# The output projection of a scan as f16 halves with a factor per chunk, one step later

## What is computed

```
x = x + 0.5 * _L0_ffn_ref(_layernorm(x, axis=-1), ...)
x = x + _L0_attn_ref(_layernorm(x, axis=-1), ...)
x = x + 0.5 * _L0_ffn_ref(_layernorm(x, axis=-1), ...)

def _L0_attn_ref(hidden_states, ...):
    h = rmsnorm(hidden_states, ln1_w)
    h = res + mamba2(h, w_in, conv_w, conv_b, A_log, D, dt_bias, w_out)
    h2 = rmsnorm(h, ln2_w)
    return h + silu(h2 @ gate_w.T) * (h2 @ up_w.T) @ down_w.T

def mamba2(...):
    ...
    y = Y.reshape(B, L, D_INNER) * silu(z)
    return y @ w_out.T
```

## Time and profile before

| | before |
|---|---|
| three runs, us | 766.61, 768.95, 770.06 |
| median, us | 768.95 |
| profiled execution, us | 768.65 |
| its span, us | 766.9 |
| PE busy in the span, us | 755.4 |
| DVE, ACT, POOL busy, us | 626.5, 446.4, 337.2 |
| the scan's sixteen steps, us from the span's start | 87.38 to 333.00 |

### The profile page before, as it was taken

One profiled execution on the slowest core, in us unless ns is written; L12 is line 12 of the kernel. 1 busy time (PEld: TensorE's weight loads), 2 busy tenths in 40 slices (PEclk: granted clock), 3 DMA queues, 4 the chain that ended last, 5 costly groups with the idle time before them and its releaser, 6 DMA issues.

```text
span 766.9 us, 10654 instructions
## 1 busy us (share of the span) xinstructions
PE 755.4 (98%) x3469; PEld 353.2 (46%) x3470; DVE 626.5 (82%) x1230; ACT 446.4 (58%) x881; POOL 337.2 (44%) x392
## 2 busy tenths in 40 slices
PE   8999999999999999999999999999999999999998
PEld 3444554454555444444443444444444444444443
DVE  6888878878878979878799978878878878767994
ACT  3877767766686766643545556456456456444441
POOL 5631534663442379775413333233233233224574
PEclk9999999999999999999999999999999999999999
DMA  8843543552321211420521743743743743443565
GB/s 311 171 75 71 139 94 83 110 111 60 78 56 28 42 38 42 114 55 1 124 47 23 172 77 64 163 77 62 164 77 65 162 77 66 79 77 69 119 169 138
DMA packets 95414, 71.86 MB, mean 94 GB/s; under 512 B 65232, under 2 KB 72400, under 8 KB 95360
## 3 DMA queue, kind: packets, MB, share of 16 engines
q0 software_dynamic: 17280, 31.46, 23.0%
q1 hardware_dynamic: 77600, 39.66, 19.5%
q10 hardware_dynamic: 480, 0.07, 0.1%
HBM read 20.32 MB, written 4.19 MB: 32 GB/s over the span
## 4 chain that ended last, share of the span: by engine, by line
PE 77%; DVE 13%; ACT 4%; issue 3%; POOL 2%; DMA 1%; ACTq 0%; POOLq 0%; DVEq 0%
PE PS L1960 64%; PE PS L2083 4%; PE PS L2183 3%; DVE raw L1450 2%; PE PS L2091 1%; DVE stage L1450 1%; PE PS L2056 1%; DVE state L1432 1%; PE PS L2065 1%; DVE st L1289 1%; PE PS L2073 1%; PE PS L2048 1%; DVE xs L1382 1%; DVE S L1415 1%; DMA h<-lora_b_t 1%
## 5 line engine op out<-in xcount | busy, mean ns | idle before, releaser
L712 POOL DMA_DIRECT2D xs<-x x59 | 50.9, 864 | 151.2 <-ACT x L1159 137.1
L1960 PE MATMUL PS<-h,w_in 128*128 128x512 f16 x480 | 108.7, 379 | 0.2 <-issue 0.2
L1960 PE MATMUL PS<-h,x_t 128*128 128x512 f16 x408 | 94.0, 379 | 0.0
L1960 PEld LDWEIGHTS PS<-h,w_in 128*128 128x128 f16 x480 | 46.9, 98 | 65.3 <-issue 15.5
L1960 PE MATMUL PS<-n_T,stage 128*128 128x512 f16 x288 | 71.5, 379 | 0.0
L1159 ACT ACTIVATE x<-PS,d_d 128x512 f32<-128x512 f32 x59 | 40.2, 682 | 39.1 <-PE PS L1960 39.1
L1960 PEld LDWEIGHTS PS<-h,x_t 128*128 128x128 f16 x408 | 39.5, 98 | 48.5 <-issue 2.3
L521 POOL TENSOR_TENSOR r<-mv,mhalf 128x1 f32<-128x1 f32 (+1 forms) x32 | 29.4, 917 | 72.2 <-DVE mv L1293 55.0
L712 POOL DMA_DIRECT2D xs<-n x29 | 25.2, 868 | 71.1 <-ACT n L1159 60.8
L1960 PE MATMUL PS<-pre,stage 128*128 128x512 f16 x192 | 49.3, 379 | 0.0
L1129 ACT ACTIVATE xds<-tm,dgh 128x512 f32<-128x512 f32 x24 | 17.3, 722 | 53.0 <-DVE tm L1889 53.0
(11 more groups left out here) (314 smaller groups left out, 1819.3 us busy)
## 6 DMA issues: line engine op xcount, KB each, us to landing
xs<-x POOLq DMA_DIRECT2D x75, 256.0 KB, 3.3
xs<-n POOLq DMA_DIRECT2D x29, 256.0 KB, 3.3
x_t<-x_in SPq DMA_DIRECT2D x16, 256.0 KB, 3.0
x_t<-hb POOLq DMA_DIRECT2D x16, 256.0 KB, 3.8
out<-x_t SPq DMA_DIRECT2D x16, 256.0 KB, 2.3
raw_gu<-gate_t SPq DMA_DIRECT2D x7, 512.0 KB, 4.4
raw_gu<-up_t SPq DMA_DIRECT2D x7, 512.0 KB, 6.6
raw_d<-down_t SPq DMA_DIRECT2D x7, 512.0 KB, 7.3
```

Source lines behind the costliest of these rows:

```text
L712: po.dma_start(chunk_of(xs, c), d_tmps[d % 3], accum_op=ALU.add).then_inc(s_acc[d % 3], 16)
L1960: ins = pe.matmul(out_, lhs(a, b, k), rhs(a, b, k), start=first and n == 0, stop=last and n == len(todo) - 1)
```

## The change

`w_out` is held as two f16 halves, scaled by a power of two, and so is y, for which each chunk and row finds a factor of its own. ACT squares y and sums over its columns (`y_sum`), PE sums over the partitions and spreads the sum (`y_over`, a matmul 128x1), DVE reads it (`y_max`), POOL takes powers (`y_scale`: the factor and its inverse), ACT makes the high half (`y_hi`) and DVE the low one (`y_lo`). The projection `w(c)` becomes one `product` of twelve f16 matmuls, and `residual2` multiplies by the inverse factor.

This chain takes longer than the step has room for, so w(c-1) is done in step c, and `residual2`, `square`, `renorm`, `rms2`, `hi2`, `lo2` and `t2` of a chunk each move one step later. `s2_inner(c)` now waits for `y_max(c-1)`, which reads the bank that it writes. In the steps 12 to 15, `y_max`, `y_hi` and `y_lo` of a chunk stand in its own step, w still in the next, and w(15) behind the first gate/up product after the scan. In the prologue the raw `w_out` is loaded later and to another place, and ACT and DVE make its scale and halves (`wo_sum`, `wo_scale`, `wo_hi`, `wo_lo`). Some links between instructions of one engine take another form.

```diff
-        w_out = sb("w_out", [P, H, DM])
+        w_out = sb("w_out", [P, 2, H, DM], F16)
 ...
+            if c > 0:
+                put(("w", c - 1), (e_x2, c), None if i + 1 < NS else B_P[2])
             if i + 1 < NS:
-                put_proj(i + 1, SLOTS[j][0])
+                for q in SLOTS[j]:
+                    put_proj(i + 1, q)
 ...
+            def y_scale(c):
+                po.wait_ge(e_ym, c + 2)
+                po.tensor_tensor(y_s[:, c, :], y_m[:, c, :], halves[:, :], ALU.pow).then_inc(e_yscale, 1)
 ...
+            def y_sum(c):
+                ac.wait_ge(e_y, c + 1)
+                if c > 1:
+                    ac.wait_ge(e_ssq, c - 1)
+                ac.activation(junk[:, :].rearrange("p (h t) -> p h t", h=H), y_of(c), ACT.Square, accum_out=ssy[:, c:c + 1]).then_inc(e_ysum, 1)
+
+            def y_hi(c):
+                ac.wait_ge(e_yscale, c + 1)
+                if c > 0:
+                    ac.wait_ge(e_wo, c)
+                ac.activation(y_hl[:, 0, :, :], y_of(c), ACT.Copy, scale=y_s[:, c, 0:1]).then_inc(e_yhi, 1)
 ...
+            def y_max(c):
+                ve.wait_ge(e_yall, c + 1)
+                ve.tensor_scalar(y_m[:, c, :], PS[:, B_SS, 0:1].broadcast_to([P, 2]), Y_TINY, None, ALU.max).then_inc(e_ym, 1)
+
+            def y_lo(c):
+                cols = slice((c % CH) * P, (c % CH + 1) * P)
+                ve.wait_ge(e_yhi, c + 2)
+                ve.scalar_tensor_tensor(y_hl[:, 1, :, :], szs[(c // CH) % 2][:, :, cols], y_s[:, c, 0:1], y_hl[:, 0, :, :],
+                                        ALU.mult, ALU.subtract).then_inc(e_ylo, 1)
 ...
-                ve.tensor_tensor(x2[:, j % 2, :], n1[:, :], bank(PLAN["w", c][0]), ALU.add).then_inc(e_x2, 1)
+                ve.scalar_tensor_tensor(x2[:, j % 2, :], bank(PLAN["w", c][0]), y_s[:, c, 1:2], n1[:, :], ALU.mult, ALU.add).then_inc(e_x2, 1)
 ...
+                if 0 < c <= 3 * CH:
+                    y_max(c - 1)
                 if c == 2 * CH + 2:
                     bound_row(0)
 ...
+                    y_lo(c - 1)
                     slot_b(i_late, late[0])
 ...
             def w(c):
                 b, freed = PLAN["w", c]
-                y = szs[(c // CH) % 2]
-                if c == 0:
-                    pe.wait_ge(s_wout, 16)
-                pe.wait_ge(e_y, c + 1)
+                pe.wait_ge(e_ylo, H + c + 1)
                 pe.wait_ge(*freed)
-                for h in range(H):
-                    last = pe.matmul(bank(b), y[:, h, (c % CH) * P:(c % CH + 1) * P], w_out[:, h, :], start=h == 0, stop=h == H - 1)
-                last.then_inc(e_wo, 1)
+                product(bank(b), lambda a, b, h: y_hl[:, a, h, :], lambda a, b, h: w_out[:, b, h, :], H).then_inc(e_wo, 1)
+
+            def y_over(c):
+                pe.wait_ge(e_ysum, c + 2)
+                pe.wait_ge(e_state, c + 1)
+                pe.matmul(PS[:, B_SS, 0:1], ssy[:, c:c + 1].broadcast_to([P, P]), over[:, :], start=True, stop=True).then_inc(e_yall, 1)
 ...
                     s1_bc(c + 1)
+                if c > 0:
+                    w(c - 1)
                 if i + 1 < NS:
                     proj(i + 1, SLOTS[j][0])
 ...
-                w(c)
                 if c == 2 * CH + 2:
                     csm(i + 1)
 ...
-                    for q in SLOTS[j][1:]:
+                    for n, q in enumerate(SLOTS[j][1:]):
                         proj(i + 1, q)
+                        if n == 0:
+                            y_over(c)
```

More of the change, by code:

```diff
@@ L209, in build @@
         wv = sb("wv", [P, 2, H])
+        y_hl = sb("y_hl", [P, 2, H, P], F16)
+        over = sb("over", [P, 1])
+        halves = sb("halves", [P, 2])
+        ssy = sb("ssy", [P, NCH])
+        y_m = sb("y_m", [P, NCH, 2])
+        y_s = sb("y_s", [P, NCH, 2])
+        wo_s = sb("wo_s", [P, 4])
         PS = ctx.enter_context(nc.psum_tensor("PS", [P, 8, 512], F32))
@@ L574, in _ @@
             chain(po.memset(ones3[:, :], 1.0))
+            chain(po.memset(over[:, :], 2.0 ** (-2 * Y_TOP)))
+            chain(po.memset(halves[:, 0:1], -0.5))
+            chain(po.memset(halves[:, 1:2], 0.5))
             chain(po.memset(ident[:, :], 0.0))
@@ L715, in _ @@
                 step(c)
-            for n in range(4, N_TOP):
+            rms2(NCH - 2, CH - 2)
+            for n in range(2):
+                t_op(2, n)
+            rms2(NCH - 1, CH - 1)
+            for n in range(2, N_TOP):
                 t_op(2, n)
@@ L939, in step @@
                     slot_b(i_late, late[0])
+                if 0 < c <= 3 * CH:
+                    y_hi(c - 1)
                 if a + 1 < NCH:
@@ L954, in step @@
                     hi1(a, a % CH)
+                y_sum(c)
                 if c + 1 < NCH:
@@ L969, in step @@
                     gate_a(0, j)
+                    y_hi(c)
                     gate_b(0, j)
-                square(c, j)
+                if c > 0:
+                    square(c - 1, (c - 1) % CH)
                 if i + 1 < NS:
@@ L1417, in scan1, with wo_scale, wo_lo @@
                 last.then_inc(e_S, 1)
+            def y_max(c):
[6 more added lines that the diff above has]
+                                        ALU.mult, ALU.subtract).then_inc(e_ylo, 1)
+            def wo_scale():
+                top, pw_, sw_, back = (wo_s[:, n:n + 1] for n in range(4))
+                ve.wait_ge(e_ysum, 1)
+                power_of_two(pw_, sw_, top, chain)
+                chain(ve.tensor_scalar(back, pw_, d_ih[:, :], 2.0 ** -W_TOP, ALU.mult, ALU.mult))
+                ve.sem_inc(e_ym, 1)
+            def wo_lo(h):
+                ve.wait_ge(e_yhi, 1)
+                ve.scalar_tensor_tensor(w_out[:, 1, h, :], wo_raw[:, h, :], wo_s[:, 2:3], w_out[:, 0, h, :],
+                                        ALU.mult, ALU.subtract).then_inc(e_ylo, 1)
             def gate_y(c, j):
@@ L1731, in step @@
                 else:
+                    y_max(c)
                     gate_up(0, j)
-                if j != 2 or i + 1 == NS:
-                    residual2(c, j)
+                    y_lo(c)
                 if c == 3 * CH:
@@ L1806, in _ @@
                 step(c)
-            lo2(NCH - 1)
             def down(i):
@@ L1923, in _ @@
             gate_lo(0, EARLY_GU)
+            lo2(NCH - 1)
             gate_up(0, EARLY_GU + 1)
```

148 lines of the change are left out of this document (89 added, 59 removed).

## The result

The changed kernel took 808.56 us in the median of four runs (807.36 to 809.6), the kernel before 767.78 us beside it: a ratio of 1.0535 (1.0516 to 1.0554). It is slower by 41 us, five times what was forecast, and outside the range.

A forecast was written before the change was run, and what follows sets the result against it. PE, busy 98% of the span, was taken to bound the kernel. 768.65 us less 13.4 for projections, plus 3.2 for y_over, less 2.3 old waits, plus 20.6 new waits gave 777 us, range 763 to 787.

The forecast's parts named there:

- the saving: Scan on PE: each chunk's projection falls from 3.43 to 2.59 us, 13.4 us over sixteen chunks.
- the lower bound that was given: PE's added y_over per chunk: 0.14 us at least, 0.38 at most; sixteen cost 2.2 to 6.1 us, taken as 3.2.
- The wait for y_lo: PE at w(c-1) in the scan stands until DVE's y_lo is done: 20.55 us in all, mainly steps 2, 6, 7, 9-11.
- Rival A: Scan: PE keeps its pace because DVE and ACT start earlier too; about 759 us, chance 0.17.
- rival B: Scan: only the latest place, y_lo(9) in step 10, holds PE; about 770 us, no change, chance 0.20.
- C: Scan: y_lo meets POOL's product in each chunk and takes 1.55 us instead of 0.75; 787 us, chance 0.10.
- DVE's wait for the maxima: Step 10: DVE's reading of the scale maxima waits about 5.0 us for a PE product behind w(9) and a projection block.
- the residual's accumulating transfer on POOL shifts by the same step: Each chunk's residual transfer on POOL moves one step later, as the transposing loads do; no cost in the sum.
- at full granted clock throughout: Scan before the change: PE works 243.33 of 245.62 us at full clock; no cost for a lower clock was forecast.
- the sign that was named: Scan, if right: PE's busy time falls by 10 us to 233 and idle time grows to some 20 us.
- I cost this at nothing: After the scan the last w stands behind one gate/up unit: no cost, bound 0 to 3 us.
- ACT's and POOL's additions I cost at nothing by themselves: Per chunk, two ACT passes (y_sum, y_hi) and one small POOL power: no cost, since ACT is idle 42% of the span.

The follow-up runs named there:

- the shift alone: Changed kernel with the f32 projection of before and no halves, factors or y passes, but still one step later and ahead of the first in-projection block: 787.17 us.
- the kernel of 788.84 us: Changed kernel with y_max, y_scale, y_hi, y_lo at the end of the chunk's own step, w(c-1) behind the first in-projection block and the maxima's spreading earlier: 788.84 us.
- the run with the other bank: Changed kernel with the third in-projection block of steps 2, 6 and 10 taking the first block's bank: 803.89 us, ratio 1.0468.
- the kernel of 789.2 us: Changed kernel with w behind the first in-projection block, early maxima spreading, POOL's sums late, w(14) and residual2(14) moved back, maxima in w(8)'s bank: 789.2 us.

## Why the prediction was wrong

**What held.** PE's full share made the saving real: the projection takes 2.59 us. y_over takes 0.14 us from start to start, the lower bound that was given. The wait for y_lo came in the places named as the main ones: 3.31 us in step 2 and 2.99 in step 6 (3.35 and 3.1 forecast), 3.15 in step 9, 6.28 in step 10, 2.46 in step 11 (2.3). Rival A and rival B fell with these rows. C fell too: the median of y_lo is 0.75 us in both rows of its line, and the longest 1.84.

```profile
L1482 DVE SCALAR_TENSOR_TENSOR y_hl<-stage,y_s,y_hl x8: 737/752/1839, 105.4 to 316.0; 128x512 f16<-128x512 f32 x8
L1482 DVE SCALAR_TENSOR_TENSOR y_hl<-raw,y_s,y_hl x8: 744/746/1423, 179.8 to 366.6; 128x512 f16<-128x512 f32 x8
```

That these waits sum to 22.1 us where 20.55 was said is partly luck. Step 7 waits 0.39 us instead of 2.35, and step 3 not at all instead of 0.8; step 8 waits 2.03 us instead of 0.95, and steps 9 and 10 together 9.4 instead of 6.75. (The pass ahead of y_lo in steps 7 and 11, read as 0.6 us long, lasts 0.69; that is too little to matter.) In step 10 three of DVE's small softplus passes met passes of POOL and took 3.6 us longer (below). DVE's wait for the maxima came, but was longer than the 5.0 us, since PE itself waits for y_lo ahead of them:

```profile
284.93 0.16 DVE L1575 COPY mxa<-PS 128x3 f32<-128x3 f32 x1 [7.14 <-PE PS L2219]
```

**What failed.** First, the step "the residual's accumulating transfer on POOL shifts by the same step", with which everything behind w was costed at nothing. Residual2 also frees a PSUM bank. The order of the banks was in the change, and I did not walk it: 8.8 us of waits in the changed kernel and 10.2 in the shift alone, where 9 us came back with w at its old place and the banks in the old order. Second, the price of a wait. I read "at full granted clock throughout" and kept that clock for the kernel after: the products behind the waits ran at the lower level and cost 14.4 us, two thirds as much as the waits for y_lo themselves. So PE's busy time in the scan did not fall to 233 us, the sign that was named, but is 244.08, and its idle time there is 35.5 us, not some 20. Third, "I cost this at nothing" for the end of the scan: the old w(15) was filler between two products, and without it PE waits 2.1 us, with 1.7 us of slow products behind, above the bound of 3:

```profile
366.70 6.99 PE L2048 MATMUL PS<-h,x_t 128*128 128x512 f16 x24 [2.11 <-DVE pre L1882]
```

Fourth, "ACT's and POOL's additions I cost at nothing by themselves". Leaving out y_sum, y_over, y_max and y_scale took 14 us off the kernel of 788.84 us, and only 2.2 of these are PE's own work.

The sign was right, and so was the wait for y_lo; as an account of the loss the mechanism was incomplete. The three rows of the table that the forecast held at nothing make up 31.9 of the 40.0 us. The wait that was forecast is also not the cause by itself, as the forecast had it. When it was taken away (22.1 to 0.3 us), 12 us came back; when the shift was made without it, 20 us were lost. The prices found in the runs do not add up to 41 us, since each was measured with other parts in place. The experiments show a program in which ACT, DVE and POOL arrive just in time in many places, above all from step 10 on: a step of delay on one of them shows up at whichever place has the least slack.

## What to carry to other kernels

A product that is moved takes its buffer's rotation with it: walk which product gets each bank next and what frees it, as carefully as the data's own waits. Price a wait of PE with the slow products behind it, here about 1.6 us for each of the nine waits that made the clock fall, and look at what the moved work used to fill at its old place. Here 13 us saved on the busiest engine were worth nothing, since their price was a chain of six small passes per step over four engines, which are on time only just.

## What was not expected of the hardware

Not every wait makes the clock fall. In the changed kernel w ran at full clock behind a wait of 2.99 us (200.51) and partly at the lower one behind 3.15 us (256.55); a block behind 2.28 us took 4.45. In step 2, w behind the same wait of 3.31 us took 4.12 us in the changed kernel and 2.76 in the run with the other bank. Whether the clock falls is not read from the wait alone, so the forecast of a single wait's price is uncertain by some 1.7 us.

A small pass can be held as long as a large one. In step 10 of the changed kernel POOL's passes of 512 columns, two of the MLP's sums and one of the scan (L559), stand beside DVE's softplus pieces of 16:

```profile
271.42 1.82 DVE L1675 SCALAR_TENSOR_TENSOR sp<-sp 128x16 f32<-128x16 f32 x1
...
271.76 1.43 POOL L675 TENSOR_TENSOR hn<-h 128x512 f32<-128x512 f16 x1
273.27 1.64 POOL L675 TENSOR_TENSOR h2n<-h 128x512 f32<-128x512 f16 x1
...
273.82 1.12 DVE L1678 SCALAR_TENSOR_TENSOR sp<-sp 128x16 f32<-128x16 f32 x1
...
274.99 1.26 POOL L559 TENSOR_TENSOR stage<-stage,ecs 128x512 f32<-128x512 f32 x1
275.06 1.22 DVE L1683 SCALAR_TENSOR_TENSOR dt<-sp 128x16 f32<-128x16 f32 x1
```

Three passes that take 0.17 us elsewhere take 4.2 us together, each ends 0.03 to 0.05 us behind the POOL pass beside it, and y_lo(9) stands right behind them. The rule of the Trainium skill that the prediction weighed (page "SBUF — State Buffer", section "Who interferes with whom") agrees in that each of the three has two SBUF inputs, and POOL's passes read SBUF; which of a pair started first these rows do not settle, since the first DVE row begins 0.34 us ahead of POOL's. The change brought two of the three pairs together by putting half of POOL's sums ahead in its step. With the sums at its end, in the kernel of 789.2 us, the second and third of these passes take 0.16 and 0.17 us again, and the first, beside the scan's pass, 1.94. The forecast looked for this at y_lo and found it in passes that the change does not touch.
